# Relative attention of a one-core transformer stack: high and low parts in f32r products, constants loaded in another order

## The reference

```python
x = (inputs - mu) / jnp.sqrt(var + LN_EPS) * ln_gamma + ln_beta
q = (x @ Wq + bq).reshape(B, S, H, dh)        # S = 1536, H = 4, dh = 16
k = (x @ Wk + bk).reshape(B, S, H, dh)
v = (x @ Wv + bv).reshape(B, S, H, dh)
p = (pe @ Wpos).reshape(S, H, dh)             # pe: positional encoding
content_score = jnp.einsum('bshd,bthd->bhst', q + u_bias, k)
pos_score = rel_shift(jnp.einsum('bshd,thd->bhst', q + v_bias, p))
score = (content_score + pos_score) / np.sqrt(D)
attn = jax.nn.softmax(score, axis=-1)
ctx = jnp.einsum('bhst,bthd->bshd', attn, v).reshape(B, S, D)
return ctx @ Wout + bout
```

## Time and profile before

| | |
|---|---|
| median of 3 runs | 5069.07 us |
| the profiled execution, its own time | 5058.97 us |
| its span, first to last instruction | 5056.8 us |
| mean granted TensorE clock | 0.882 |
| busy share PE / PEld / DVE / ACT / POOL | 80% / 53% / 55% / 45% / 10% |
| DMA traffic | 26.52 MB, mean 5 GB/s |

### The profile page before, as it was taken

One profiled execution on the slowest core, in us unless ns is written; L12 is line 12 of the kernel. 1 busy time (PEld: TensorE's weight loads), 2 busy tenths in 40 slices (PEclk: granted clock), 3 DMA queues, 4 the chain that ended last, 5 costly groups with the idle time before them and its releaser, 6 DMA issues. The chain is left out here.

```text
span 5056.8 us, 70418 instructions
## 1 busy us (share of the span) xinstructions
PE 4046.9 (80%) x26656; PEld 2691.9 (53%) x26656; DVE 2799.3 (55%) x6139; ACT 2255.8 (45%) x3803; POOL 494.5 (10%) x824
## 2 busy tenths in 40 slices
PE   6786866799887876799887775799887876799888
PEld 4664644465546544365546554365546554365546
DVE  4555737355555738355555648455545747455544
ACT  3343648254342548254342558254342549244332
POOL 0000010201100010201100010201100010201100
PEclk9898977899898987899898887899898987899988
DMA  2000000000000000000000000000000000000000
GB/s 89 3 3 17 1 17 1 1 1 1 1 1 4 1 17 1 0 1 1 1 1 4 1 18 1 0 1 1 1 1 4 1 1 1 1 1 1 1 1 4
DMA packets 28313, 26.52 MB, mean 5 GB/s; under 512 B 10550, under 2 KB 26934, under 8 KB 27450
## 3 DMA queue, kind: packets, MB, share of 16 engines
q1 hardware_dynamic: 27962, 21.98, 1.5%
HBM read 20.40 MB, written 1.57 MB: 4 GB/s over the span
## 5 line engine op out<-in xcount | busy, mean ns | idle before, releaser
L720 ACT ACTIVATE big<-ps,negmax 128x1024 f32<-128x1024 f32 (+1 forms) x672 | 600.1, 899 | 266.1 <-DVE negmax L753 266.0
L706 ACT COPY big<-ps 128x512 f32<-128x512 f32 x672 | 394.1, 586 | 493.2 <-PE ps L647 490.1
L753 DVE TENSOR_REDUCE negmax<-ps 128x1 f32<-128x1536 f32 x336 | 589.9, 1758 | 38.2 <-PE ps L623 18.5
L647 PE MATMUL ps<-cst,big 128*128 128x128 f32 x4032 | 502.7, 275 | 30.4 <-ACT big L720 29.9
L647 PEld LDWEIGHTS ps<-cst,big 128*128 128x128 f32 x4032 | 457.2, 142 | 48.5 <-ACT big L720 40.5
L424 PE MATMUL ps<-cst 128*128 128x512 f32 x608 | 310.0, 666 | 128.4 <-DVEq L190 58.2
L437 ACT COPY xt<-ps 64x512 f32<-64x512 f32 x144 | 78.9, 579 | 710.7 <-PE ps L429 710.6
L616 PE MATMUL ps<-kup,qup 128*128 128x512 f32 (+3 forms) x768 | 359.2, 565 | 41.8 <-POOLq L190 41.0
L409 POOL TENSOR_TENSOR st<-st,cst 128x6 f32<-128x6 f32 x104 | 156.8, 1508 | 2187.1 <-DVE st L397 2183.0
L663 PE MATMUL ps<-big,v 128*32 128x128 f32 (+1 forms) x8064 | 321.9, 277 | 8.1 <-DVE ctxt L1244 6.0
L616 PE MATMUL ps<-klo,qlo 128*128 128x512 f32 (+3 forms) x672 | 313.7, 550 | 3.6 <-DVE big L706 1.6
(11 more groups left out here) (394 smaller groups left out, 7239.0 us busy)
## 6 DMA issues: line engine op xcount, KB each, us to landing
rw<-in_w_route SPq DMA_DIRECT2D x128, 64.5 KB, 1.8
cst<-in_consts SPq DMA_DIRECT2D x1, 2671.0 KB, 14.6
cst<-in_consts SPq DMA_DIRECT2D x1, 2670.5 KB, 8.7
big<-in_consts SPq DMA_DIRECT2D x1, 1872.5 KB, 21.7
out_dram<-res SPq DMA_DIRECT2D x4, 384.0 KB, 2.9
experts_in<-in_consts SPq DMA_DIRECT2D x1, 1360.0 KB, 17.4
qup<-in_patches SPq DMA_DIRECT2D x4, 260.0 KB
klo<-in_pe_low SPq DMA_DIRECT2D x2, 384.0 KB, 23.1
```

Source lines behind the costliest of these rows:

```text
L647: ins = nc.tensor.transpose(turned_bank(kind, u, g)[:, i * P:(i + 1) * P], prob[:, slot_of(kind, u), (4 * g + i) * P:(4 * g + i + 1) * P], ...
L706: copy(pt[:, slot_of(kind, u), g, 0:n], turned_bank(kind, u, g)[:, 0:n]).then_inc(*ph.mark(copier(kind, g)))
L720: nc.scalar.activation(prob[:, slot_of(kind, u), cols], src[:, cols], ACT.Exp, bias=bias, accum_out=part_sum[:, u, k:k + 1]).then_inc(*ph. ...
L753: nc.vector.tensor_reduce(negmax[:, u:u + 1], flat[:, 0:n], AX.X, ALU.max, negate=True)\
```

## The change

Scores of attn3 become sums of f32r products. A bank is now one product of 64 rows of `k_stack` (content and low-part terms; rows 0 to 63 for the first head of the pair, 64 to 127 for the second) and, for each of its `klo` and `kup` parts, two products of 128 rows: `q_stack` or `q_more` (turned queries, high rows and low rows) with the high and with the low part of the position table. `side` becomes four such products. POOL's `qz` copies go.

rel3a and rel3b spread the weights on DVE first (`w_stack`, `w_pos`, in `big`). The query product L1725 now yields 16 rows, the key product becomes a stack of 128 rows for content and keys, and the turning products take 16 rows of `qv` and yield 128. ACT writes the high parts (`k_stack`, `turned_high`) and moves them by one column (`moved_up`); DVE makes the low parts and the sum that POOL made.

Constants come in the order of use, under three semaphores: a first part for the embedding, the position tables, then all else, awaited in route0. The rounding of the expert weights, the bias work and the copies for the spread go to route0, and `load_experts(0)` goes to the start.

```diff
-                if kind.startswith("attn3"):
...
-                    nc.gpsimd.tensor_copy(qz[64:80, u % 2, :], qlo[64:80, hd % 2, q * P:(q + 1) * P])\
-                        .then_inc(*ph.mark("queries_alone"))
...
                     s = hd % 2
                     cut = min(max(q, lo), hi)
-                    parts = [(lo, cut, qlo, klo), (cut, hi, qup, kup)]
-                    parts = [(a, b, qq, kk) for a, b, qq, kk in parts if a < b]
-                    for a, b, qq, kk in parts:
-                        ins = nc.tensor.matmul(bank[:, (a - lo) * P:(b - lo) * P], qq[:, s, qs], kk[:, s, a * P:b * P],
-                                               start=True, stop=True)
+                    rows = slice(D * s, D * s + D)
+                    nc.tensor.matmul(bank[:, 0:(hi - lo) * P], k_stack[rows, 0, qs].bitcast(F32R),
+                                     k_stack[rows, 1, lo * P:hi * P].bitcast(F32R), start=True, stop=False, skip_group_check=True)
+                    for a, b, qq, kk in ((lo, cut, q_stack, klo), (cut, hi, q_more, kup)):
+                        for w in range(2 if a < b else 0):
+                            ins = nc.tensor.matmul(bank[:, (a - lo) * P:(b - lo) * P], qq[:, s, qs].bitcast(F32R),
+                                                   kk[:, w, a * P:b * P].bitcast(F32R), start=False, stop=(w == 1),
+                                                   skip_group_check=True)
...
-                n = min(P + 1, S - q * P)
-                nc.tensor.matmul(ps[:, 7, 0:P], qlo[:, s, qs], klo[:, s, qs], start=True, stop=True)
-                pe.wait_ge(*ph.after("queries_alone", u + 1))
-                nc.tensor.matmul(ps[:, 7, P:P + n], qz[:, u % 2, :], klo[:, s, q * P:q * P + n], start=True, stop=True)\
-                    .then_inc(*ph.mark("side_ready"))
+                n = min(P + 2, S - q * P)
+                rows = slice(D * s, D * s + D)
+                nc.tensor.matmul(ps[:, 7, 0:P], k_stack[rows, 0, qs].bitcast(F32R), k_stack[rows, 1, qs].bitcast(F32R),
+                                 start=True, stop=False, skip_group_check=True)
+                for w in range(2):
+                    nc.tensor.matmul(ps[:, 7, 0:P], q_stack[:, s, qs].bitcast(F32R), klo[:, w, qs].bitcast(F32R),
+                                     start=False, stop=(w == 1), skip_group_check=True)
+                nc.tensor.matmul(ps[:, 7, P:P + n], k_stack[rows, 0, qs].bitcast(F32R),
+                                 k_stack[rows, 1, q * P:q * P + n].bitcast(F32R), start=True, stop=True,
+                                 skip_group_check=True).then_inc(*ph.mark("side_ready"))
 
...
-            sp.dma_start(cst[:, 0:half], consts[:, 0:half]).then_inc(consts_in, 16)
-            sp.dma_start(cst[:, half:EXPERT_AT], consts[:, half:EXPERT_AT]).then_inc(consts_in, 16)
-            sp.dma_start(experts_in[:, :], consts[:, EXPERT_AT:SETUP_AT]).then_inc(consts_in, 16)
-            sp.dma_start(setup_in[:, 0:CONST_COLS - SETUP_AT], consts[:, SETUP_AT:CONST_COLS]).then_inc(consts_in, 16)
...
-            sp.dma_start(kup[0:D, 0, :], pe_up).then_inc(consts_in, 16)
-            sp.dma_start(kup[0:D, 1, :], pe_up).then_inc(consts_in, 16)
...
+            sp.dma_start(cst[:, 0:EARLY], consts[:, 0:EARLY]).then_inc(first_in, 16)
+            sp.dma_start(setup_in[0:DH, 0:2 * S], consts[0:DH, SETUP_AT:SETUP_AT + 2 * S]).then_inc(first_in, 16)
+            sp.dma_start(setup_in[:, 2 * S:CONST_COLS - SETUP_AT], consts[:, SETUP_AT + 2 * S:CONST_COLS]).then_inc(first_in, 16)
+            load_tokens(0)
+            for part in range(2):
+                sp.dma_start(pe_in[D * part:D * part + D, 0, :], pe_low).then_inc(tables_in, 16)
+                sp.dma_start(pe_in[D * part:D * part + D, 1, :], pe_up).then_inc(tables_in, 16)
+            sp.dma_start(route_sb[:, :], route).then_inc(route_in, 16)
+            sp.dma_start(cst[:, EARLY:half], consts[:, EARLY:half]).then_inc(consts_in, 16)
+            sp.dma_start(cst[:, half:ROT_AT], consts[:, half:ROT_AT]).then_inc(consts_in, 16)
+            for part in range(2):
+                sp.dma_start(cst[D * part:D * part + D, ROT_AT:ROT_AT + 2 * S], consts[0:D, ROT_AT:ROT_AT + 2 * S]).then_inc(consts_in, 16)
+            sp.dma_start(cst[:, ROT_AT + 2 * S:EXPERT_AT], consts[:, ROT_AT + 2 * S:EXPERT_AT]).then_inc(consts_in, 16)
+            sp.dma_start(experts_in[:, :], consts[:, EXPERT_AT:SETUP_AT]).then_inc(consts_in, 16)
...
+            sp.wait_ge(route_in, 16)
+            load_experts(0)
...
-            sp.wait_ge(route_in, 16)
-            load_experts(0)
...
+            act.wait_ge(consts_in, CONST_DMAS)
+            nc.scalar.copy(big[D:P, 0:SETUP_AT - EXPERT_AT].bitcast(F32R), experts_in[D:P, :]).then_inc(*ph.mark("rounded"))
...
+            nc.scalar.copy(experts[0:D, :].bitcast(F32R), experts_in[0:D, :])
...
+                    def turned_high(i):
+
+                        s, j = i // NB, i % NB
+                        act.wait_ge(*ph.after("sum_ready", i + 1))
+                        nc.scalar.copy(q_stack[:, s, 512 * j:512 * (j + 1)].bitcast(F32R), rt1[:, i % 2, :])\
+                            .then_inc(*ph.mark("turned_high"))
+
+                    def moved_up(i):
+
+                        s, j = i // NB, i % NB
+                        c, o = 512 * j, 1 if j == 0 else 0
+                        act.wait_ge(*ph.after("turned_low", i + 1))
+                        nc.scalar.copy(q_more[:, s, c - 1 + o:c + 511].bitcast(F32R), q_stack[:, s, c + o:c + 512])
+
...
-                        for content in (qlo, qup):
-                            ins = nc.scalar.activation(content[64:80, s, cols], ps[64:80, bank, :], ACT.Identity,
-                                                       bias=bias3[64:80, hd:hd + 1], scale=0.125)
-                        ins.then_inc(*ph.mark("content_ready"))
+                        act.wait_ge(*ph.after("stack_psum", i + 1))
+                        nc.scalar.copy(k_stack[:, w, cols].bitcast(F32R), ps[:, bank + 1, :]).then_inc(*ph.mark("high_ready"))
+                        if i >= 1:
+                            turned_high(i - 1)
+                        if i >= 2:
...
-                            pe.wait_ge(*ph.after("k_copied", i - 1))
-                            pe.wait_ge(*ph.after("content_ready", i - 1))
-                        nc.tensor.matmul(ps[0:80, bank, :], W("wq3")[:, 80 * hd:80 * hd + 80], xt[:, cols], start=True, stop=True)\
+                            pe.wait_ge(*ph.after("qv_ready", i - 1))
+                            pe.wait_ge(*ph.after("low_ready", i - 1))
+                        at = 80 * (2 * half + s)
+                        nc.tensor.matmul(ps[0:DH, bank, :], W("wq3")[:, at:at + DH], xt[:, cols], start=True, stop=True)\
                             .then_inc(*ph.mark("q_psum"))
-
-                        at = CONST_AT["wk3"][1] + DH * hd
-                        nc.tensor.matmul(ps[0:80, bank + 1, :], cst[:, at - D:at + DH], xt[:, cols], start=True, stop=True)\
-                            .then_inc(*ph.mark("k_psum"))
+                        nc.tensor.matmul(ps[:, bank + 1, :], w_stack[0:65, s, :, :, :].rearrange("p s k c -> p (s k c)"), xt[0:65, cols],
+                                         start=True, stop=True).then_inc(*ph.mark("stack_psum"))
...
-                            w = W("wpos3")[:, (2 * hd + r) * D:(2 * hd + r + 1) * D]
-                            ins = nc.tensor.matmul(ps[0:D, bank + 2 + r, :], w, qv[:, i % 2, :], start=True, stop=True)
+                            w = w_pos[0:DH, i // NB, r, :, :].rearrange("p k c -> p (k c)")
+                            ins = nc.tensor.matmul(ps[:, bank + 2 + r, :], w, qv[0:DH, i % 2, :], start=True, stop=True)
...
-            rough = big[:, 0:SETUP_AT - EXPERT_AT]
-            nc.vector.tensor_copy(rough.bitcast(F32R), experts_in[:, :])
+            dve.wait_ge(tables_in, TABLE_DMAS)
+            for w, keys in enumerate((klo, kup)):
+                nc.vector.tensor_copy(keys[:, 0, :].bitcast(F32R), pe_in[:, w, :])
             nc.vector.drain()
-            nc.vector.tensor_tensor(experts[D:P, :].bitcast(F32R), experts_in[D:P, :], rough[D:P, :], ALU.subtract)
-            nc.vector.tensor_copy(experts[0:D, :].bitcast(F32R), experts_in[0:D, :])
-
-            for rows in (xt[D:P, :], mean_t[D:P, :], w1s[D:P, :, :], klo[D:P, :, :], kup[D:P, :, :], qz[:, :, :]):
-                nc.vector.memset(rows, 0.0)
-            nc.vector.drain()
-            nc.vector.memset(xt[D:D + 1, :], 1.0)
-            nc.vector.memset(mean_t[D:D + 1, :], 1.0)
+            for w, keys in enumerate((klo, kup)):
...
+            dve.wait_ge(*ph.after("bias_psum", 1))
+            nc.vector.tensor_copy(bias_row[D:D + 1, :, :].rearrange("p e c -> p (e c)"), ps[64:65, 2, 0:HEADS * D])
+            dve.wait_ge(*ph.after("rounded", 1))
+            nc.vector.tensor_tensor(experts[D:P, :].bitcast(F32R), experts_in[D:P, :], rough[D:P, :], ALU.subtract)
...
```

(61 more changed lines are left out.)

98 lines of the change are left out of this document (54 added, 44 removed).

## The result

The changed kernel takes 5365.38 us (median of 4 runs, 5356.64 to 5384.18) against 5066.62 for the kernel before: 1.0599 times, interval 1.0571 to 1.0626. 5184 was forecast, in a range of 5020 to 5250. The direction was right; the loss is 299 us where 115 were expected. The profiled execution has a span of 5360.1 us, 303 more than before, at a mean granted clock of 0.844 (0.882 before).

A forecast was written before the change was run, and what follows sets the result against it. DVE's loop in attn3 bound at 5.83 us a unit, PE's own work 5.64 close behind. Terms +142 +10 +2 -27 -12 = +115 on 5058.97 gave 5174, median 10 higher: 5184 us, range 5020 to 5250.

The forecast's parts named there:

- The price of a change of rows: attn3 scores: each change between 64 and 128 rows costs 0.21 us; a unit 6.57 against 5.83, +142 us in all.
- the first rival: attn3: changes of rows cost nothing, DVE's loop binds at 5.50 a unit, -63 us; total 4967; chance 0.11.
- rel3 at 3.95 a step: rel3: three shape changes lengthen a step from 3.74 to 3.95 us, +10 us over 48 steps.
- the clock as a rival: attn3: short PE stops drop the clock to 1.2 GHz a fifth of its time; about 5370 us; chance 0.04.
- At the stage starts the clock is lower and a change no cheaper, so I leave the 16 starting units in: attn3 stage starts: the 16 starting units count at the same +0.74 us as the others, within the 192 units.
- Start and route0: Constants' loading and routing: embed starts on DVE at 25 instead of 52, -27 us; route0 ends earlier, -12 us.
- the pace of rel3's steady steps: rel3: DVE about 3.3 and ACT some 2.5 us a step, both staying under PE's 3.95.
- the end of rel3: rel3's end: PE's wait goes from 5.13 to 4.7 us, counted as -0.4 for each of 8 stages.

## Why the prediction was wrong

- **The price of a change of rows: right.** 0.21 a change gave 6.57 a unit; 6.58 was measured, with single distances of 0.42, 0.67 and 1.00 where 0.43, 0.66 and 1.00 were forecast, and with the changes taken out DVE's loop came down to the 5.50 that the first rival had for it. In rel3 the forecast wrote 3.95 a step, and the one step at full clock took 3.93; but the terms as they stand there, 3.43 + 0.30 + 0.03 + 0.22, add to 3.98, so the nearer fit is in part a slip of the sum.
- **rel3 at 3.95 a step: wrong, and the largest term.** The step that failed reads "3.43 + 3 x 0.10 + 0.03 + 2 x 0.11 = 3.95, so +0.21 x 48 steps = +10"; it took for granted that the passes stay at 0.43. They went to 0.85, because the granted clock stood at 0.50, and rel3 cost +156; the old kernel over fewer rows shows that the narrow products are what holds it there. I counted the clock as a rival, with 0.04, but only for attn3, from short stops of PE. That its 5370 lies next to the measured 5365 is chance: it was worked out for a fifth of attn3 at half clock, and the loss lies in rel3, which fell to 0.50 in a stream without a stop. The Trainium skill, page "TensorE: Matmul & The Clock Gate", section "What's actually happening", ties the gate to how busy the PE has been; by it a PE busy 40.00 of 40.00 us keeps 2.4 GHz. The trace has 0.50 there, and so the measurement decides.
- **"At the stage starts the clock is lower and a change no cheaper, so I leave the 16 starting units in": wrong by size.** Behind rel3 the clock is at 0.50 in both kernels. Before, it is back 3.0 to 6.0 us after the first score product. With f32r products of which a third has 64 rows it stays at 0.50 for 16.8 to 18.5 us in the kernel of the row below, and for 16.8 to 26.8 in the changed kernel:

```profile
951.00:964.00 13.00, 13.00 (x26) 6.33 (x26) 2.35 (x3) 1.88 (x4) 0.20 (x1) 0.50 0.00 1
```

  This is the kernel with 128-row turning products, so it isn't the turning products' doing; without 64-row products the clock is back after 4.0 to 4.2. The first two intervals between units (from one last side product to the next) are 7.07 and 7.05 to 7.79 there, 3.03 to 3.13 and 5.60 before, 2.65 and 5.34 without 64-row products: together 14.55, 8.67 and 7.99 on average. Over eight stages this is (14.55 - 8.67) x 8 = 47 over before, of which I had 12. Against the run without them it is (14.55 - 7.99) x 8 = 52, of which the expected 207 held 17: 35 of the 42 us by which its gain of 249 exceeded 207.
- **Start and route0: right,** -40.2 against -39, in two parts of -28.8 and -11.4.
- **The first rival was wrong as a statement on the chip, and right as one on the design:** where there is no change of rows, three f32r products a bank beat two float32 passes by 0.33 a unit.
- DVE and ACT never set the pace of rel3's steady steps (3.74 with all their new work and one change fewer), and the end of rel3 costs PE a stop of 4.87 in all eight stages (5.13 in the earlier trace rows, 4.7 forecast); it is 5.34 with 128-row turning products.

The part of the account that is argued and not shown: that the late clock at the start of attn3 and the fall in rel3 have one cause. In both, products of few rows run while the clock is low, and both end when the rows are filled. But the same products of attn3 had the clock back anywhere between 16.8 and 39.5 us, and lost it twice for 3.4 us in the middle of a stage, so with 64-row products among them something else has a say in when it changes, and no run here shows what. The -6 us outside rel3, attn3, start and spread are not explained either.

## What to carry to other kernels

A contraction cut down to the rows that carry data saved nothing on TensorE here, and cost twice: once when products of 64 and of 128 rows alternate, and once more when a stage of narrow products kept the clock down for as long as it lasted. Keep the rows of zeros, or pad with them, and read the granted clock by stage before and after. Where a stage's clock could change, its whole length is the term at risk, not its added instructions: here rel3's clock had no chance of its own and made half of the loss. The better kernel came from the parts: three f32r products at full height and the new order of loading, 4977 us.

## What the runs showed of the hardware

- The granted clock fell from 1.00 to 0.50 in a stream without a gap. Products of 128 x 16, 65 x 128 and 16 x 128 (rows x outputs) lost or never regained it, as did 64 x 80, 65 x 80 and 16 x 64; 128 x 80, 65 x 128 and 16 x 128 regained it for 3 to 10 us and lost it; 128 x 80, 128 x 80 and 16 x 64 kept it, as did 128 x 16, 65 x 128 and 128 x 128 once it was up. The weights in the added rows were zeros (in the key product the data), and the clock was kept for them all the same: it is the rows of the instruction that count, not what they hold.
- Behind a stop of 5 us the granted clock was back 3.0 to 6.0 us after the first product where all had 128 rows, and after 14.7 to 39.5 us where a third of the f32r products had 64 rows, with PE busy throughout.
- A change of the weights' shape costs a stream of products some 0.15 to 0.21 us: 0.42 for a 64-row product among 128-row ones, where a stream of one shape needs 0.23, and 0.11 more for the pair behind it; 0.19 for 16 x 128 behind 65 x 128; some 0.15 for 128 x 80 to 128 x 64, where only the outputs change; nothing for 65 x 128 to 128 x 128 (0.43 from start to start). The kernel before paid it in rel3 already.
